# Attention and experts kernel: scores from slot 0 on, first attention scores, router logits and projections of q and v in the drain, q split behind k, operand loads in two separate halves

## What is computed

```python
xn = _layernorm(x, axis=-1)                      # x: (8, 512, 128)
x = x + attn(xn) + ffn(xn)
# attn: 16 heads of 8, causal, softmax, output projection with bias
scores = jnp.einsum('bhqd,bhkd->bhqk', q * scale, k) + causal_bias
out = jnp.einsum('bhqk,bhkd->bhqd', softmax(scores), v)
# ffn: softmax router over 8 experts, the top 2 scaled by 2.5, plus a shared expert
g = silu(einsum('td,edf->etf', x, w_gate)) * einsum('td,edf->etf', x, w_up)   # F = 176
y = einsum('te,etd->td', combine, einsum('etf,efd->etd', g, w_down))
y = y + swiglu(x, sw_gate, sw_up, sw_down)       # 352 hidden
```

## Time and profile before

| | us |
|---|---|
| median of 3 runs (lowest, highest) | 663.87 (661.8, 669.11) |
| the profiled execution | 668.29 |
| its span in the profile | 666.6 |
| TensorE busy | 571.7 (86%) |
| VectorE busy | 474.5 (71%) |
| ScalarE busy | 347.9 (52%) |
| GpSimd busy | 358.6 (54%) |

### The profile page before, as it was taken

How to read it: one execution, slowest core, us unless ns; L and a number is a source line. 1 busy time by engine, 2 the same in 40 slices (tenths; PEclk the granted TensorE clock), 3 DMA queues, 4 the chain that set the end, 5 groups by cost and what they waited for, 6 DMA issues and landing times.

```text
span 666.6 us, 12739 instructions
## 1 busy us (share of the span) xinstructions
PE 571.7 (86%) x4208; PEld 324.8 (49%) x4208; DVE 474.5 (71%) x821; ACT 347.9 (52%) x472; POOL 358.6 (54%) x338
## 2 busy tenths in 40 slices
PE   1249989999799989999799988999899988989794
PEld 1136652556336643466336653466425663366422
DVE  4956967589756967479765988479664897569613
ACT  1422359533883448633693349634595338733482
POOL 3425726477257733478265754478154872568342
PEclk9658989999999988999999999999899999999879
DMA  6946004830247002850049001750039202670000
GB/s 162 267 104 165 1 7 97 195 75 16 55 127 189 16 6 51 179 133 16 21 109 239 16 6 47 188 128 16 6 95 213 54 16 53 143 176 16 7 1 17
DMA packets 44438, 57.12 MB, mean 86 GB/s; under 512 B 5936, under 2 KB 29840, under 8 KB 44240
## 3 DMA queue, kind: packets, MB, share of 16 engines
q1 hardware_dynamic: 44416, 56.83, 35.6%
HBM read 41.60 MB, written 15.20 MB: 85 GB/s over the span
## 4 chain that ended last, share of the span: by engine, by line
PE 63%; DVE 16%; issue 6%; DMA 5%; SPq 5%; ACT 4%; POOL 0%; DVEq 0%; POOLq 0%; ACTq 0%
PE banks L586 8%; PE banks L452 7%; PE banks L454 6%; PE banks L453 6%; PE banks L483 6%; PE banks L465 6%; PE banks L558 4%; PE banks L474 4%; PE banks L467 3%; PE banks L466 3%; DVE neg_max L1067 3%; ACT probs L768 2%; DMA k_op<-k_dram 2%; PE banks L608 2%; SPq L344 2%
## 5 line engine op out<-in xcount | busy, mean ns | idle before, releaser
L1067 DVE TENSOR_REDUCE neg_max<-banks 128x2 f32<-128x1024 f32 (+3 forms) x224 | 194.0, 915 | 39.1 <-PE banks L474 37.6
L855 POOL TENSOR_SCALAR_AFFINE_SELECT probs<-probs 128x512 f32<-128x512 f32 x128 | 92.8, 748 | 157.7 <-ACT probs L768 157.7
L768 ACT ACTIVATE probs<-banks 128x1024 f32<-128x1024 f32 x160 | 155.7, 1025 | 12.9 <-PE banks L558 10.7
L728 ACT ACTIVATE probs<-banks 128x512 f32<-128x512 f32 (+1 forms) x112 | 67.0, 598 | 163.8 <-PE banks L454 163.1
L822 POOL TENSOR_TENSOR probs<-probs,cb 128x512 f32<-128x512 f32 x88 | 116.3, 1322 | 67.0 <-ACT probs L728 54.7
L828 POOL TENSOR_TENSOR hid_lo<-probs,hid_hi 128x512 fp32r<-128x512 f32 (+1 forms) x96 | 123.2, 1284 | 52.7 <-ACT hid_hi L736 51.8
L586 PE MATMUL banks<-probs,v_op 128*32 128x512 f32 (+3 forms) x1024 | 97.0, 452 | 0.2
L452 PE MATMUL banks<-x_hi,w_hi 128*128 128x512 f32 (+1 forms) x224 | 93.5, 417 | 2.7 <-DVE w_lo L1203 2.7
L736 ACT ACTIVATE hid_hi<-probs 128x512 fp32r<-128x512 f32 (+1 forms) x112 | 69.5, 628 | 39.8 <-DVE probs L1049 39.6
L454 PE MATMUL banks<-x_hi,w_lo 128*128 128x512 f32 (+1 forms) x224 | 90.0, 402 | 0.0
L453 PE MATMUL banks<-x_lo,w_hi 128*128 128x512 f32 (+1 forms) x224 | 89.5, 400 | 0.0
(11 more groups left out here) (113 smaller groups left out, 644.1 us busy)
## 6 DMA issues: line engine op xcount, KB each, us to landing
cb<-c_dram SPq DMA_DIRECT2D x32, 256.0 KB, 7.8
q_op<-q_dram SPq DMA_DIRECT2D x32, 192.0 KB, 5.6
k_op<-k_dram SPq DMA_DIRECT2D x32, 192.0 KB, 6.2
cb<-c_dram SPq DMA_DIRECT2D x16, 224.0 KB, 8.1
q_dram<-q_parts SPq DMA_DIRECT2D x16, 192.0 KB, 2.7
k_dram<-k_parts SPq DMA_DIRECT2D x16, 192.0 KB, 2.7
cb<-c_dram SPq DMA_DIRECT2D x16, 192.0 KB, 7.9
cb<-c_dram SPq DMA_DIRECT2D x16, 160.0 KB, 6.4
```

The lines of the kernel that those rows point to most:

```text
L768: nc.scalar.activation(probs[:, g % 2, 2 * u:2 * u + 2, :], ring[:, 2 * (n % 2):2 * (n % 2) + 2, :], ACT.Exp).then_inc(exp_done, 1)
L855: return nc.gpsimd.affine_select(out=view, in_=view, compare_op=ALU.is_ge, fill=0.0, base=0, pattern=[[0, 4], [1, P]], channel_multiplier=-1)
L1067: return nc.vector.tensor_reduce(out, in_, AX.X, ALU.max, negate=True)
```

## The change

- Scores: one pair in slots 0 to 3, two in slots 4 to 11, none in 12. Pairs 0 to 3 use banks 3 and 4, later ones alternate. Pair 4 waits for the attention output's addition of the row before, which now stands in `nat` (the transpose of the normalised o and the output projection moved there).
- Drain: the maxima's transpose stands ahead of `down(11)`. After `project_k` come `logits` (now in bank 4), the first two units of `scores_t` around `down(12)` and `down(13)`, then `project_q` and `project_v`. `transpose_y` comes after unit (0,3). ScalarE loads the table of exponentials before it copies the maxima, and copies y after its second exponential. LATE is 3.
- VectorE: `router_logits` between the last low parts; `split_k`, `split_q`, `take_v` ahead of tokens and router weights.
- SyncE: the first half of the operands is read ahead of the router's weights, the second behind them.
- Tiles `hid`, `sg`, `yT`, `att`, `both` lie in other parts of `probs`; the ring's two double banks swap roles in attention, so `gate_up(0)` waits for all 20 exponentials, where it waited for 19.

```diff
-LATE = 2
+LATE = 3
 EARLY = 2
 
-PAIRS_AT = [(int(2 <= k <= 12), int(4 <= k <= 12)) for k in range(16)]
-SPARE_FROM = 4
+AHEAD = 0
+PAIRS_AT = [1 if k < 4 else 2 if k < 12 else 0 for k in range(NT + 2)]
+ONE_SLOT = AHEAD + 4
 
 
 def pair_slot(n):
 
-    return (n - SPARE_FROM) % 2 if n > SPARE_FROM else 0
+    return n % 2 if n >= ONE_SLOT else 1
...
-        hid = probs[:, 0, 0:3, :]
-        sg = probs[:, 0, 3:6, :]
-        yT = probs[:, 0, 6, :]
-        att = probs[:, 0, 7, :].rearrange("p (q e) -> p q e", q=QT)
-        both = probs[:, 0, 8, :].rearrange("p (q e) -> p q e", q=QT)
+        att = probs[:, 0, 0, :].rearrange("p (q e) -> p q e", q=QT)
+        both = probs[:, 0, 1, :].rearrange("p (q e) -> p q e", q=QT)
+        hid = [probs[:, 0, n, :] for n in (4, 6, 2)]
+        sg = [probs[:, 0, n, :] for n in (5, 7, 3)]
+        yT = probs[:, 0, 8, :]
...
+        o_banks = [bank_y, bank_m, bank_y, banks[:, 5, :]]
...
                 k_parts_out(i + 1)
                 q_parts_out(i + 1)
+                operands_in(i + 1, i, 0)
                 weights_out(i + 1)
                 weights_around(FIRST_SEGMENTS, cb_loaded)
-                operands_in(i + 1, i)
                 weights_around(OTHER_SEGMENTS, cb_others)
+                operands_in(i + 1, i, 1)
...
-                before(pe, base_done, j)
+                pe.wait_ge(router_step, ROUTER_STEPS * j + 2)
...
-                before(pe, y_taken, j)
...
-                    mm = pe.matmul(bank_y[:, q * NE:(q + 1) * NE], xnT[:, q * P:(q + 1) * P], gate_sb[:, :],
...
-                n = 0
+                n = 0 if i is None else AHEAD
                 for k in range(NT + 2):
                     if k < NT and (k >= 2 or i is None):
                         gate_up(b, k)
                     if k == 2 and i is not None:
                         transpose_o(i, 3, True)
-                    for _ in range(sum(PAIRS_AT[k])):
-                        scores(b, i, n // NAT_PAIRS, n % NAT_PAIRS)
+                    for _ in range(PAIRS_AT[k] + (AHEAD if k == 0 and i is None else 0)):
+                        pair(b, i, n)
                         n += 1
-                    if k == NT and front:
-                        project_k(b + 1)
+                    if k == NT - 1:
+                        transpose_maxima(b)
+                        if front:
+                            transpose_x(b + 1)
+                    if k == NT:
+                        if front:
+                            project_k(b + 1)
+                            logits(b + 1)
+                        scores_t(b, 0, 0)
+                    if k == NT + 1:
+                        scores_t(b, 0, 1)
                     if k >= 2:
                         down(b, k - 2, i)
                     if k == 2 and i is not None:
                         transpose_on(i)
                     if k == 3 and i is not None:
                         project_out(i)
-                    if k == 13:
-                        transpose_maxima(b)
-                        if front:
-                            transpose_x(b + 1)
+                if front:
+                    project_q(b + 1)
+                    project_v(b + 1)
 
             def attend(i, front):
-                transpose_y(i)
                 for g in range(GROUPS + 1):
                     for u in range(UNITS):
-                        if g < GROUPS:
+                        if g < GROUPS and (g, u) not in ((0, 0), (0, 1)):
                             scores_t(i, g, u)
+                        if (g, u) == (0, 3):
+                            transpose_y(i)
                         if front and g == GROUPS and u in (2, 3):
                             gate_up(i + 1, u - 2)
...
                         if front:
-                            if (g, u) == (0, 0):
-                                logits(i + 1)
-                            if (g, u) == (0, 1):
-                                project_v(i + 1)
-                            if (g, u) == (0, 2):
-                                project_q(i + 1)
...
+
+                        nc.scalar.activation(table_call[:, :], bqk[:, 1:2], ACT.Exp)
...
-                high_hidden(b, NT - 1)
+                        nc.scalar.activation(o_normT[:, :], nat[:, 0, :], ACT.Copy).then_inc(onT_done, 1)
                 if front:
                     take_k(b + 1)
-                act.wait_ge(down_done, NT * b + NT)
+                high_hidden(b, NT - 1)
+
+            def take_y(i):
+                act.wait_ge(down_done, NT * i + NT)
                 nc.scalar.activation(yT[:, :], bank_y[:, :], ACT.Copy).then_inc(y_taken, 1)
-
-                nc.scalar.activation(table_call[:, :], bqk[:, 1:2], ACT.Exp)
...
+                        if g == 0 and 1 <= u <= 3:
+
+                            act.wait_ge(hid_lo_done, NT * i + NT - 3 + u)
+                        if g == 0 and u == 4:
+                            act.wait_ge(yback_ready, i + 1)
+                        at = 2 * ((n + 1) % 2)
+                        nc.scalar.activation(probs[:, g % 2, 2 * u:2 * u + 2, :], ring[:, at:at + 2, :], ACT.Exp
                                              ).then_inc(exp_done, 1)
+                        if (g, u) == (0, 1):
+                            take_y(i)
                         if front:
-                            if (g, u) == (0, 1):
+                            if (g, u) == (0, 0):
                                 exp_router(i + 1)
                             if (g, u) == (0, 2):
                                 take_q(i + 1)
...
-                    if k == 12:
+                    if n == NAT_ALL and PAIRS_AT[k]:
                         split_maxima(b)
-                    if k == 12 and front:
+                    if n == NAT_ALL and not PAIRS_AT[k] and PAIRS_AT[k - 1] and front:
                         normalise(b + 1)
                     if k == 6 and i is not None:
                         find_numbers(i)
                     if k == 8 and i is not None:
                         finish_output(i)
-                for k in range(NT - LATE, NT):
-                    low_hidden(b, k)
+                    if k >= NT - LATE + 2:
+                        low_hidden(b, k - 2)
+                if front:
+                    router_logits(b + 1)
+                low_hidden(b, NT - 1)
 
             def attend(i, front):
+                if front:
+                    split_k(i + 1)
+                    split_q(i + 1)
+                    take_v(i + 1)
                 add_tokens(i)
                 if front:
-                    router_logits(i + 1)
-                    split_k(i + 1)
-                    take_v(i + 1)
                     router_weights(i + 1)
                 take_o(i, 0)
                 if front:
-                    split_q(i + 1)
                     take_combT(i + 1)
                 normalise_o(i, 0)
```

121 lines of the change are left out of this document (58 added, 63 removed).

## The result

| | before | after |
|---|---|---|
| median, us | 665.98 (661.8 to 669.11, 4 runs) | 731.25 (729.92 to 731.58, 4 runs) |
| profiled execution, us | 668.29, span 666.6 | 729.92, span 728.2 |
| mean granted clock | 0.955 | 0.910 |

The changed kernel takes 1.098 times as long, with a 95% interval of 1.091 to 1.105. I had forecast 694 us and a range up to 712. The sign and the wait for comb came out as written; the size did not, and 731 lies outside the range.

The account below looks back on a forecast made before the run. TensorE was taken as nearly full in experts and attention, VectorE as tight in the experts. 668.3 + 23.1 + 1.5 - 1.5 + 7 = 698.4 us profiled, 694 median; range 678 to 708, 8 in 10 672 to 712.

Parts of the forecast that it names:

- the wait for comb: Attention stage: TensorE waits 4.2 us at the transpose of the router's weights, in seven rows.
- the 3.3 counted: Attention stage: the transpose of comb comes at 415.4 instead of 412.14, +3.3 us in each of seven rows.
- The front: Slots 0 and 1: the third tile starts 2.4 us late, slot 4's 1.39 us wait goes; sum 0.
- The rest of the experts: Experts stage to slot 13: VectorE is tight, hidden(11) ends at about 391.9, gate/up 13 starts +0.3 us.
- The sum 26.3 for VectorE's work: Experts stage: attention add, 8 hidden products, 16 maxima, two tail operations and 0.5 us idle, ending at 389.5.
- The drain: Behind the experts: scores_t(0,0) idles 1.3 us for the maxima, scores_t(0,2) ends 403.6; ScalarE gains 0.9 us.
- The chain: Attention stage: the q split, ahead of v, tokens and router, waits for q until 405.8; comb ready at 415.3.
- The clock term: Behind seven comb waits: lower clock, 1.7 us per drop, 0 to 12 us; 9 taken, less 2, so 7.
- the 2 off for disturbed periods of before: Whole span: the fuller drain may spare the disturbed periods of the kernel before, 2 us off.
- First and last row: First row +1.5 us from postponed tiles behind the operand wait; last attention, without router, keeps the drain's gain, -1.5.
- The split loads: SyncE's queue: reading the operands' first half ahead of the router's weights gives nothing.

Follow-up runs that it names:

- run 8: The changed kernel with hidden(11) put ahead of the split of the row maxima on VectorE again: 706.93 us, ratio 1.057.
- Run 4: The changed kernel with three throwaway projections ahead of the transpose of comb and eight throwaway matmuls ahead of scores_t(0,0): 694.69 us, ratio 1.039.
- run 9: The changed kernel with both halves of the operand load side by side again, behind the router's first weight group: 730.89 us, ratio 1.094.
- run 6: Run 5's kernel with q projected right behind the logits, its bias added earlier, and the token add behind the router: 656.7 us, ratio 0.980.
- run 7: The changed kernel with only the table of score slots of before put back: 704.56 us, ratio 1.051; the second time 705.2 us, ratio 1.053.
- run 5: The changed kernel with the first two attention score units moved back behind down 12 and down 13: 706.64 us, ratio 1.055.
- run 11: Run 6 with the slot table of before, plus throwaway matmuls in two waits ending the experts: 645.04 us; or down 11 moved ahead of the transposes: 686.64 us.
- x in slot 1: Run 6 with hidden(11) ahead of the maxima's split and the next row's normalised x moved into slot 1 on VectorE: 657.28 us, ratio 0.983.

## Why the prediction was wrong in size

In short: against the forecast of 698.4 us for the profiled execution 31.5 us are missing. The low clock, put at 9 us, costs some 35 in the trace, and that is 26 of them. The term failed by leaving out the drain, where new idle time ahead of dense work was given no price, and by taking the drop at comb too small. Most of the rest is 1 us per row more than the 3.3 counted (85.14 - 75.39 less 5.5 of clock is 4.3).

**The front: right but for a microsecond.** Pair 1 waits 1.33 us (said: 1.4). Tile 2 starts at 306.33, or 356.22 on the prediction's clock (said: 356.2). Tiles 4 and 5 start at 363.65 and 366.89, about one microsecond later than said (362.8, 365.8).

**The rest of the experts: mis-sized.** The step said that hidden(11) ends at 391.9 and gate/up 13 starts there, +0.3 us. It starts at 393.32, 1.75 us later than before and behind a wait of 1.72. The order of causes was right (the split of the maxima, one of whose casts takes 1.15 us where its twin takes 0.20, as in the earlier trace rows, stands ahead of hidden(11)). The sum 26.3 for VectorE's work held; it began the microsecond later that the front was late. But run 8 shows that the wait itself isn't what it costs: taken away, it came back at the next place, and the 24 us that the edit did bring were mostly the drain's clock.

**The drain: its own steps right, its clock missed.** The maxima's trips took 4.29 us from the end of the copy to scores_t(0,0) (said: 4.1), and the wait there was 1.84 (said: 1.3). From there the step counted 4.3 us to scores_t(0,2), all durations taken from the rows of a full clock. It took 7.26. The step that failed is the unspoken one: it laid down an idle 1.3 us ahead of the drain's dense work and gave it no price, though the next paragraph priced just that at comb. Run 4 shows it: with TensorE kept busy ahead of it, the same list of instructions takes 4.17. ScalarE's first exponential came at 401.85 (said: 399.8), exponential 2 at 408.98 (said: 404.0).

**The chain: right.** q done at 360.69 to comb at 369.58 is 8.9 us (said: 9.6); the transpose waits 3.58 us in seven rows (said: 4.2). Because scores_t(0,2) was 4.9 us later than said (408.46 against 403.6), its place shifted but hardly its size: TensorE too reaches it later.

**The clock term: wrong by a factor of four.** I took 1.7 us per drop, 9 in all (7 with the 2 off for disturbed periods of before, which came to 5.8), and 12 at most. Its size came from one stretch of 3.6 us at 0.54. Measured are two drops per row: 2.3 to 2.5 us at comb (first column, 14.92 against 12.54 in the row shown) and in the drain, against run 4's 4.17, 1.6 us in the first two rows and 2.9 to 3.1 in the other five. That is some 35 over the seven; run 4 gives 36.6. Two things failed in it: the size of a drop was taken from a single case of 3.6 us, where the low clock of the row shown holds for most of 7.8 us in the drain and for all of 5.4 us behind comb; and drops were counted only behind the wait that I was looking at.

One sign of this lay in the trace of before. The two long periods that the prediction calls disturbed (77.93 and 77.89 us) have the low clock in the drain:

```profile
244.80:255.10 10.30, 9.61 (x38) 5.45 (x36) 5.81 (x13) 6.15 (x9) 0.84 (x1) 0.67 0.01 5
```

The waits ahead of it (1.19, 0.71 and 0.69 us) are those of the undisturbed rows. The prediction looked for a drop in the undisturbed row alone; in the other two it costs 2.5 us.

The Trainium skill (TensorE: Matmul & The Clock Gate, HAM oscillation) describes this pattern, a kernel whose waits let the clock fall and whose next burst starts cold each time, with long waits for a transfer in its example. This case's trace agrees on the pattern and shows it at shorter ones: 1.84 us in the drain, with 1.72 and 0.84 a little ahead of it. My prediction used that page only to bound the comb wait.

**First and last row.** From the first to the second transpose of comb the changed kernel takes 76.64 us (before 69.93). That is 6.7, and a later row's difference without its first column is 85.14 - 75.39 - 2.38 = 7.4, so the first row comes out 0.7 lower (said: 1.5 higher). The drain's clock is the reason: the fourth column is 5.78 there instead of 7.26. The experts up to scores_t(0,0) are 0.3 us longer than before in this row (56.07 against 55.80), where a later row's are 0.6 shorter, so the front by itself did cost 0.8. TensorE waited longer there for its first operands than before:

```profile
49.82 0.61 PE L485 MATMUL banks<-k_op,q_op 48*128 48x512 bf16 x2 [5.79 <-DMA k_op<-k_dram]
```

Behind the last transpose of comb it is +1.4 (said: -1.5). Of that 2.5 is the low clock behind the seventh wait for comb (15.00 us to gate/up 0 instead of 12.54), which belongs to the clock term; the rest is -1.0, close to what was said. No projections of a next row stand between the maxima and the first scores there, so the trips through memory are waited for in full; even so scores_t(0,0) comes 51.8 us behind gate/up 0, before 52.6:

```profile
692.37 0.61 PE L558 MATMUL banks<-q_op,k_op 51*128 51x512 bf16 x2 [4.96 <-DMA q_op<-m_dram]
```

**The sum again.** 668.3 of the profiled execution; less 5.8 for the longer periods of before (76.20, 77.93 and 77.89 against 75.39), since the changed kernel's periods are all alike; plus 6.7 for the first row, 59.2 for the six that follow (511.57 against 6 x 75.39), and 1.4 for the end: 729.8, measured 729.9.

**The split loads: right.** They give nothing (run 9).

**What stays open.** What decides where the clock falls. The wait of 1.33 us at pair 1 has the low clock behind it in one row of the changed kernel, in six rows of run 9 and in none of run 6. The kernel of run 7 had it in the drain in one execution and in the experts in another. The clock fell behind the comb wait of 3.5 to 3.6 us in every row of every run that has it, but stayed up behind the single one of 2.47 (run 5). And whether a real piece of work can take the place of the throwaway matmuls that make the fastest version.

## What to carry to other kernels

Price a new wait of TensorE together with the work right behind it: idle times of 1.8 and 3.6 us cost up to another 3.1 and 2.5 us in the dense stretches that followed, and all waits ahead of such a stretch count, also the small ones that the change brings by the way. If an operation is moved ahead on an in-order engine, its producer must be moved ahead first: the same split of q cost 42 to 46 us when q came late, and left no wait at comb once q was projected and biased a few instructions sooner. And where an edit that should win a few microseconds moves the time by three times as much or not at all, compare the granted clock of the stretches before looking for another queue.

## What the runs showed of the hardware

- Filling waits with useless matmuls made the kernel faster: with 98 more matmul records 36.6 us less (run 4), and from 656.2 to 645.0 in run 11.
- The waits behind which the clock fell are short: 1.33 and 1.70 us within 5 us in the experts (0.74, x in slot 1, in three rows of five); 1.78 and 1.35 within 2 us at the transposes (0.50); 1.84 behind 1.72 and 0.84 in the drain (0.56). With 1.72, 0.84 and 0.38 in the same places (run 6) it stayed at 1.00.
- One program can have its low stretches in different places: in the rows of one execution (before: 75.4 and 77.9 us) and from one execution to the next (run 7, 20 us).
- Of the two casts 128x64 in the split of the maxima, one takes 0.20 us and the other 1.15. In the changed kernel it is the second that is slow, in run 8 the first (1.13 and 0.20):

```profile
415.71 1.13 DVE L1090 CAST max_parts<-neg_max 128x64 bf16<-128x64 f32 x1
...
417.13 0.20 DVE L1095 CAST max_parts<-max_rest 128x64 bf16<-128x64 f32 x1
```

The slow one is, in each of the eight rows of both kernels and of the kernel before, the one that meets GpSimd's product of the hidden tile. It starts 0.21 to 0.23 us behind it and ends 0.05 us behind its end; the fast one meets no work of GpSimd. In the row above:

```profile
415.49 1.29 POOL L830 TENSOR_TENSOR probs<-probs,cb 128x512 f32<-128x512 f32 x1 [0.78 <-ACT probs L728]
```

The traces show this together each time; no run moved GpSimd's product by itself.
